# First layer of a four-layer kernel: products of tiles 0 and 1 interleaved over eight PSUM banks, with VectorE's order in tiles 1 and 2 and the place of the first down product changed

## Chip, cores and metric

The kernel runs on one core of a Trainium2 chip. The metric is the device time of one execution in microseconds (us). The kernel before takes 749.59 us, the median of 3 runs (749.37 to 749.69).

## What is computed

Four conditioned layers are applied in turn to x of 64 x 64 tokens of 256 features (4096 tokens), with one condition vector of 64 numbers per batch of 64 tokens. The change is in the first layer alone, a gated product with quantised activations and weights:

```
scale = cond @ norm_w.T + 1.0
ms = jnp.mean(x * x, axis=-1, keepdims=True)
h = x * (scale[:, None, :] * jax.lax.rsqrt(ms + EPS))
u = h @ up_w.T
val, gate = jnp.split(u, 2, axis=-1)
h = val * jax.nn.gelu(gate, approximate=False)
hq = h + jax.lax.stop_gradient(act_quant(h) - h)
wq = down_w + jax.lax.stop_gradient(weight_quant(down_w) - down_w)
y = hq @ wq.T
return y + x
```

The second layer is attention and a gated product, the third an adapter whose weights are made from the condition, the fourth a layer norm with a shift from the condition.

## The kernel before, in words

The program for each engine is written out by hand, with semaphores between engines. The first layer (`layer0`) works on 32 tiles (N) of 128 tokens. For each tile:

- GpSimd (POOL) scales the tile and splits it in a high and a low part (`split_tile`: xs L356, xs_hi L362, xs_lo L364, then semaphore xs_ready), and makes rstd0 from the tile's squares (`row_scale`, L371 and L373).
- TensorE (PE) multiplies by up_hi and up_lo (`up_chunk`, L435). A tile has four pieces of 512 columns in the order UP_ORDER: gate and value of the first half (j = 0), gate and value of the second (j = 1). Each piece takes three products, high by high, high by low and low by high, each of two matmuls, so 24 matmuls a tile. up_done counts halves.
- ScalarE (ACT) takes the gelu of the gate (`gate`, L552) and squares the tokens of a tile two ahead (`square_tokens`, L516), for which they must have been loaded.
- VectorE (DVE) multiplies gelu by the value into h (`gated`, L659, then h_done), finds the largest magnitude (`largest`, L667 to L671), rounds into q (`quantise`, L622 and L626, then q_done), and later adds the down product to the tokens as y (`add_tokens`, L614).
- SyncE (SP) issues the loads. From tile 4 on its order for tile s is: transpose of q of tile s - 3 (L272), w1_stage (L262), tokens of tile s (L259), tokens_again (L279). For tile 4 the first of these waits for q_done 2, which is q of tile 1.
- PE makes the down product of a tile (`down`, L452, 8 matmuls) two tiles later, and transposes y (`y_transposes`, L472) three tiles later.

Every engine runs its `body(s)` for s = 0, 1, 2, ... in `pipeline`; the first steps are unrolled, with special work in them. In step 0 and before it, the up weights arrive in four pieces: ACT rounds each to up_hi (L598) and DVE takes the rest as up_lo (L694). ACT sums the down weights' magnitudes (L575); in step 1 PE adds these over partitions (L488) and makes four condition vectors (L441), DVE derives the thresholds (`prepare_down`) and quantises the down weights in two steps, `below_minus_half` (L647) and `above_half` (L651). In step 2 PE makes three more condition vectors (L441), which ACT copies and turns into Tanh (L563, L589) behind its squares of the tokens of tile 4; before PE transposes the first y it waits for these (cond_done 4), because they share bank 7. y's product has bank 6.

The bank of a piece is 2j + part for every tile, so a tile can start on a half only when h of that half of the tile ahead has been made:

```
pe.wait_ge(Z["xs_ready"], t + 1)
wait(pe, Z["h_done"], 2 * s.at(1) + j + 1 if s.live(1) else 0)
```

Of the kernel before, what the change touches and what calls it, by code (L numbers as in the profile page):

```python
# [18 lines left out]
ACT = mybir.ActivationFunctionType  # L19
# [181 lines left out]
def layer0(nc, io, core, bank, sb, sem, early):  # L201
# [36 lines left out]
    stat_loaded, rstd_row = core["stat_loaded"], core["rstd_row"]  # L238
    norm_ps, down_ps, late_ps = bank[7][:, 0:DH * B], bank[7][:, 0:1], bank[7][:, DH * B:4 * DH * B]
    loaded_up, tokens_loaded, stage_loaded = ([sem(f"{n}{i}") for i in range(4)] for n in ("loaded_up", "tokens_loaded", "stage_loaded"))  # L240
# [7 lines left out]
    def sync_program(sp):  # L248
# [67 lines left out]
        load_up(3)  # L316
        load_tokens(first[1])
        sp.dma_start(down_f, io["down_t"]).then_inc(Z["loaded_down"], 16)
        sp.dma_start(core["ident"][:], io["ident"]).then_inc(Z["loaded_vecs"], 16)
        sp.dma_start(cond_w[:, (NORM + 1) * D:NV * D], io["cond_w"][:, (NORM + 1) * D:NV * D]).then_inc(Z["loaded_cond"], 16)  # L320
        sp.dma_start(vecs[:, 0:13], io["vecs"]).then_inc(Z["loaded_vecs"], 16)
        load_x(256, 512, "loaded_x1")
        for s in first:
# [75 lines left out]
    def gpsimd_program(pool):  # L399
        def body(s):  # L400
            if s.live(1):
                row_scale(pool, s, 1)
            split_tile(pool, s)
            if s.last(0):
                row_scale(pool, s, 0)
            w1_low(pool, s)
            if s.last(-1):
                attention_input(nc, pool, core, Step(0, 0, 1), 0)
                attention_input(nc, pool, core, Step(0, 0, 1), 1)
            if s.last(0):  # L410
                attention_input(nc, pool, core, Step(0, 0, 1), 2)
                attention_input(nc, pool, core, Step(1, 1, 1), 0)
                attention_input(nc, pool, core, Step(1, 1, 1), 1)
            row_scales(pool, s)
# [5 lines left out]


    def up_chunk(pe, s, j):

        t, k = s.at(0), s.slot(0, 2)
        if j == 0:
            pe.wait_ge(Z["xs_ready"], t + 1)
        wait(pe, Z["h_done"], 2 * s.at(1) + j + 1 if s.live(1) else 0)
        for part in (1, 0):
            at = part * FF + j * 512
            piece = UP_ORDER.index((j, part)) + 1  # L430
            for n, (a, b) in enumerate(((0, 0), (1, 0), (0, 1)) if s.first() else SPLITS):
                if s.first() and n != 1:
                    pe.wait_ge(Z["up_lo_done" if b else "up_hi_done"], piece)
                for d in range(DH):
                    last = nc.tensor.matmul(bank[2 * j + part][:, :], (xs_hi, xs_lo)[a][:, k, d, :], up[b][:, d, at:at + 512],  # L435
                                            start=n == d == 0, stop=n == 2 and d == DH - 1)
        last.then_inc(Z["up_done"], 1)
# [38 lines left out]
    def tensor_program(pe):  # L476
# [5 lines left out]
        def body(s):  # L482
            up_chunk(pe, s, 0)
            up_chunk(pe, s, 1)
            if s.first_tile(1):
                pe.wait_ge(Z["down_sum"], 1)
                pe.wait_ge(Z["norm_done"], 1)
                nc.tensor.matmul(down_ps, core["ones"][:], wscale[:, 0:1], start=True, stop=True).then_inc(Z["down_total"], 1)  # L488
                pe.wait_ge(Z["loaded_cond"], 16)
                for v in (GAMMA1, BETA1, ALPHA1, GAMMA2):  # L490
                    last = cond_vector(pe, v, bank[5][:, (v - GAMMA1) * DH * B:])
                last.then_inc(Z["cond_ready"], 1)
            y_transposes(pe, s)
            if s.first_tile(2):
# [3 lines left out]
                last.then_inc(Z["cond_ready"], 1)  # L498
            down(pe, s)

# [44 lines left out]
    def scalar_program(act):  # L545
        def gate(s, j):
            act.wait_ge(Z["up_done"], 2 * s.at(0) + j + 1)
            if j == 0:
                act.wait_ge(Z["rstd0_done"], s.at(0) + 1)
            wait(act, Z["h_done"], 2 * s.at(1) + j + 1 if s.live(1) else 0)  # L550
            hold(act, Z["passed"])
            nc.scalar.activation(gelu[:, j, :], bank[2 * j + 1][:, :], ACT.Gelu,  # L552
                                 scale=rstd0[:, bass.ds(s.at(0), 1)]).then_inc(Z["gelu_done"], 1)
# [12 lines left out]
        def body(s):  # L566
# [6 lines left out]
            if s.first():  # L573
                act.wait_ge(Z["loaded_down"], 16)
                nc.scalar.activation(stat[:, T // 2:T], down_f, ACT.Abs, accum_out=wscale[:, 0:1]).then_inc(Z["down_sum"], 1)  # L575
            if s.first_tile(1):
                w1_high(s, 1)
                square_tokens(act, s, -1)
            if not s.last(0) and not s.first():
                w1_high(s)  # L580
            if s.live(-2) and not s.first():
                square_tokens(act, s, -2)
            if s.first_tile(1):
                cond_vectors(GAMMA1, 4, bank[5], 1)
            if s.first_tile(2):
# [47 lines left out]
    def vector_program(ve):  # L633
# [20 lines left out]
        def gated(s, j):  # L654
            t, k = s.at(0), s.slot(0, 2)
            ve.wait_ge(Z["gelu_done"], 2 * t + j + 1)
            if j == 0:
                wait(ve, Z["q_done"], s.at(1))
            nc.vector.scalar_tensor_tensor(out=h[:, k, j * 512:(j + 1) * 512], in0=bank[2 * j][:, :], scalar=rstd0[:, bass.ds(t, 1)],  # L659
                                           in1=gelu[:, j, :], op0=ALU.mult, op1=ALU.mult).then_inc(Z["h_done"], 1)  # L660
# [12 lines left out]
        def body(s):  # L673
            add_tokens(ve, s)
            quantise(ve, s)
            gated(s, 0)
            if s.first_tile(1):
                prepare_down()
                below_minus_half()
            y_scale(ve, s)  # L680
            gated(s, 1)
            if s.first_tile(1):
                above_half()
            if s.last(0):
# [1372 lines left out]
```

## Time and profile before

| | us |
|---|---|
| Median of 3 runs | 749.59 |
| The profiled execution | 748.37 |
| Its span | 746.6 |
| PE busy | 730.2 (98%) |
| DVE busy | 518.1 (69%) |
| POOL busy | 419.5 (56%) |
| ACT busy | 363.4 (49%) |

The span is the time between the first and the last recorded event of the profiled execution. Busy counts leave out waiting and the issue of transfers. The granted clock of TensorE was 0.997 of full speed over the whole span. A matmul's recorded end is modelled, and matmuls overlap.

### The profile page before, as it was taken

The numbers are of one execution on the slowest core, as the hardware profiler recorded it, in microseconds if no ns is written. First come the engines' busy times: TensorE is split into PE (matmuls) and PEld (weight loads), VectorE is DVE, ScalarE is ACT, GpSimd is POOL, SyncE is SP. The second block draws the span as 40 slices with busy tenths as digits, with TensorE's granted clock in tenths as the row PEclk, the third lists the DMA queues.
The fourth block names the chain that finished last, engine by engine and source line by source line (L and its number), as shares of the span: only waits on it lengthen the run. The fifth ranks groups of instructions, "written<-read, shape, count | busy, mean of one in ns | idle before, by whom it ended". The sixth has DMA issues, their size and how long they took to land.

```text
span 746.6 us, 18077 instructions
## 1 busy us (share of the span) xinstructions
PE 730.2 (98%) x6406; PEld 597.5 (80%) x6406; DVE 518.1 (69%) x805; ACT 363.4 (49%) x719; POOL 419.5 (56%) x408
## 2 busy tenths in 40 slices
PE   8999999999999899999999999999999999999996
PEld 6888888888888799999988777677677767778884
DVE  3977778777789988888985464646655565553467
ACT  4444444444447687888875323333333332322585
POOL 4756646655678888999987533424242423320244
PEclk9999999999999999999999999999999999999998
DMA  8955344444433010000004355476757777759953
GB/s 244 296 108 107 86 118 106 106 120 117 99 81 74 12 36 3 2 1 0 2 4 127 76 185 178 153 243 204 203 181 246 215 223 222 243 161 389 387 179 129
DMA packets 80810, 105.69 MB, mean 142 GB/s; under 512 B 39760, under 2 KB 53168, under 8 KB 80624
## 3 DMA queue, kind: packets, MB, share of 16 engines
q1 hardware_dynamic: 79600, 103.32, 46.9%
q10 hardware_dynamic: 1152, 1.59, 1.0%
q8 instruction: 38, 0.62, 0.3%
q14 instruction: 20, 0.16, 0.1%
HBM read 75.23 MB, written 21.26 MB: 129 GB/s over the span
## 4 chain that ended last, share of the span: by engine, by line
PE 90%; DVE 3%; POOL 3%; issue 2%; DMA 1%; ACT 1%; SPq 0%; DVEq 0%; POOLq 0%; ACTq 0%
PE banks L435 23%; PE banks L1202 22%; PE banks L1232 12%; PE banks L1048 5%; PE banks L1254 4%; PE banks L1125 4%; PE banks L452 4%; PE banks L1083 3%; PE banks L1166 3%; PE banks L1141 2%; PE banks L1863 2%; PE banks L1107 2%; PE banks L1833 2%; DMA early<-in_up_t 1%; PE banks L1855 1%
## 5 line engine op out<-in xcount | busy, mean ns | idle before, releaser
L1584 DVE TENSOR_TENSOR g<-banks,silu 128x512 f32<-128x512 f32 x64 | 44.1, 689 | 79.3 <-PE banks L1202 52.0
L1424 ACT ACTIVATE g_hi<-g 128x512 fp32r<-128x512 f32 x64 | 40.4, 631 | 97.8 <-DVE g L1584 96.7
L1588 DVE TENSOR_TENSOR g_lo<-g,g_hi 128x512 fp32r<-128x512 f32 x64 | 55.0, 859 | 47.5 <-ACT g_hi L1424 47.5
L1418 ACT ACTIVATE silu<-banks 128x512 f32<-128x512 f32 x64 | 38.2, 597 | 97.9 <-PE banks L1202 97.9
L435 PE MATMUL banks<-up_hi,xs_hi 128*128 128x512 f32 x256 | 81.9, 401 | 1.3 <-POOL xs_lo L364 0.8
L435 PE MATMUL banks<-up_lo,xs_hi 128*128 128x512 f32 x256 | 79.5, 391 | 0.5 <-DVE up_lo L694 0.5
L435 PE MATMUL banks<-up_hi,xs_lo 128*128 128x512 f32 x256 | 79.2, 391 | 0.0
L1202 PE MATMUL banks<-mlp_in_hi,w_hi 128*128 128x512 f32 x252 | 78.8, 394 | 0.0
L1202 PE MATMUL banks<-mlp_in_lo,w_hi 128*128 128x512 f32 x252 | 78.0, 391 | 0.0
L1202 PE MATMUL banks<-mlp_in_hi,w_lo 128*128 128x512 f32 x252 | 77.8, 390 | 0.0
L659 DVE SCALAR_TENSOR_TENSOR h<-banks,rstd,gelu 128x512 f32<-128x512 f32 x64 | 47.9, 748 | 35.4 <-ACT gelu L552 35.2
L552 ACT ACTIVATE gelu<-banks,rstd 128x512 f32<-128x512 f32 x64 | 43.9, 686 | 43.7 <-PE banks L435 36.0
L940 POOL TENSOR_TENSOR p_sb<-p_sb,rec 128x1024 f32<-128x1024 f32 x32 | 60.7, 1905 | 7.7 <-DVE rec L1543 7.7
L724 POOL TENSOR_TENSOR mlp_in_lo<-mlp_in,mlp_in_hi 128x1024 fp32r<-128x1024 f32 x8 | 19.9, 2490 | 77.2 <-ACT mlp_in_hi L731 77.2
L435 PEld LDWEIGHTS banks<-up_lo,xs_hi 128*128 128x128 f32 x256 | 47.8, 188 | 11.7 <-DVE up_lo L694 1.7
L435 PEld LDWEIGHTS banks<-up_hi,xs_lo 128*128 128x128 f32 x256 | 48.1, 188 | 10.4
L1202 PEld LDWEIGHTS banks<-mlp_in_lo,w_hi 128*128 128x128 f32 x252 | 47.3, 188 | 10.7
L1202 PEld LDWEIGHTS banks<-mlp_in_hi,w_hi 128*128 128x128 f32 x252 | 47.2, 188 | 10.8
L1202 PEld LDWEIGHTS banks<-mlp_in_hi,w_lo 128*128 128x128 f32 x252 | 47.3, 188 | 10.3
L1232 PE MATMUL banks<-g_hi,w_hi 128*128 128x512 f32 x128 | 52.7, 412 | 2.3 <-DVE y_alpha L1597 1.7
L714 POOL TENSOR_TENSOR mlp_in<-x_sb,stat 128x1024 f32<-128x1024 f32 (+1 forms) x8 | 19.6, 2445 | 61.0 <-DMA stat<-rstd_row 43.1
L435 PEld LDWEIGHTS banks<-up_hi,xs_hi 128*128 128x128 f32 x256 | 45.6, 188 | 10.2 <-POOL xs_lo L364 0.9
(224 smaller groups left out, 1806.3 us busy)
## 6 DMA issues: line engine op xcount, KB each, us to landing
gen_hyper<-in_gen_t SPq DMA_DIRECT2D x32, 512.0 KB, 4.5
gen_made<-base_w SPq DMA_DIRECT2D x64, 256.0 KB, 4.4
adapter_w<-gen_made SPq DMA_DIRECT2D x64, 256.0 KB, 4.4
tokens<-in_x_tok SPq DMA_DIRECT2D x32, 128.0 KB, 2.4
w_stage<-in_w_t SPq DMA_DIRECT2D x32, 128.0 KB, 2.4
tokens_again<-in_x_tok SPq DMA_DIRECT2D x32, 128.0 KB, 2.3
weight_slot<-adapter_w SPq DMA_DIRECT2D x4, 1024.0 KB, 8.9
x_sb<-in_x_t SPq DMA_DIRECT2D x7, 512.0 KB, 7.1
```

The lines of the kernel that those rows point to most:

```text
L435: last = nc.tensor.matmul(bank[2 * j + part][:, :], (xs_hi, xs_lo)[a][:, k, d, :], up[b][:, d, at:at + 512], start=n == d == 0, stop=n == ...
L452: last = nc.tensor.matmul(y_ps, qt[:, s.slot(2, 2), f, :], downq[:, f, :], start=f == 0, stop=f == FC - 1)
L552: nc.scalar.activation(gelu[:, j, :], bank[2 * j + 1][:, :], ACT.Gelu, scale=rstd0[:, bass.ds(s.at(0), 1)]).then_inc(Z["gelu_done"], 1)
L659: nc.vector.scalar_tensor_tensor(out=h[:, k, j * 512:(j + 1) * 512], in0=bank[2 * j][:, :], scalar=rstd0[:, bass.ds(t, 1)], in1=gelu[:, j, ...
L940: nc.gpsimd.tensor_tensor(pu, pu, rec[:, two, :].unsqueeze(2).to_broadcast([P, 16, L]), ALU.mult).then_inc(A["norm_done"], 1)
L1048: last = nc.tensor.matmul(ps[:, m * GTA:(m + 1) * GTA], w1[a][:, w + d * D + m * P:w + d * D + (m + 1) * P], ha[b][k][:, d, :], start=n == ...
L1202: last = nc.tensor.matmul(chunk_bank(s, f, i)[:, :], w1[a][:, at:at + P], hs[b][k][:, d, :], start=n == d == 0, stop=n == 2 and d == DH - 1)
L1232: last = nc.tensor.matmul(bank[5 + m][:, :], w1[a][:, at:at + P], gs[b][:, f % 2, :], start=f == n == 0, stop=f == FC - 1 and n == 2)
L1418: nc.scalar.activation(silu[:, f % 2, :], chunk_bank(s, f, 0)[:, :], ACT.Silu).then_inc(S["silu_done"], 1)
L1424: nc.scalar.activation(gs[0][:, f % 2, :], g[:, f % 2, :], ACT.Copy).then_inc(S["g_hi_done"], 1)
L1584: nc.vector.tensor_tensor(g[:, f % 2, :], chunk_bank(s, f, 1)[:, :], silu[:, f % 2, :], ALU.mult).then_inc(S["g_done"], 1)
L1588: nc.vector.tensor_tensor(gs[1][:, f % 2, :], g[:, f % 2, :], gs[0][:, f % 2, :].bitcast(FP32), ALU.subtract).then_inc(S["g_ready"], 1)
```

## The change

In step 0 PE runs the 48 matmuls of tiles 0 and 1 in a hand-written order (`first_two_tiles`). Tile 1 has banks 4 to 7 of its own and no wait for h; its first two products stand between the high and the low products of tile 0's second piece. To feed it, POOL splits tile 1 directly after tile 0, ahead of the rstd of tile 0. The total and the first four condition vectors get other banks (3 and 2), and wait for h_done 2. Tile 2 is back in banks 0 to 3, and its second half waits for the copy of the condition vectors, which ACT makes earlier in step 1. The down product of tile 0 moves from the end of step 2 to between the two halves of tile 3. On DVE `below_minus_half` goes behind the second h of tile 1, `above_half` goes from step 1 into step 2 between the two h of tile 2, and quantising tile 1 goes behind them. On SP the load of x for tiles 2 and 3 goes ahead of the down weights.

```diff
--- before.py
+++ after.py
@@ -236,7 +236,7 @@
     lines_ps, last_lines_ps = bank[7][0:4, DH * P:DH * P + P], bank[3][0:4, 0:P]
     row_squares, row_rstd = core["rows"]
     stat_loaded, rstd_row = core["stat_loaded"], core["rstd_row"]
-    norm_ps, down_ps, late_ps = bank[7][:, 0:DH * B], bank[7][:, 0:1], bank[7][:, DH * B:4 * DH * B]
+    norm_ps, down_ps, norm_four_ps, late_ps = bank[7][:, 0:DH * B], bank[3][:, 0:1], bank[2], bank[7][:, DH * B:4 * DH * B]
     loaded_up, tokens_loaded, stage_loaded = ([sem(f"{n}{i}") for i in range(4)] for n in ("loaded_up", "tokens_loaded", "stage_loaded"))
     qt_loaded, again_loaded = ([sem(f"{n}{i}") for i in range(2)] for n in ("qt_loaded", "again_loaded"))
     names = ("loaded_norm loaded_cond loaded_vecs loaded_down loaded_x0 loaded_x1 loaded_x norm_ready norm_done cond_ready cond_done "
@@ -315,11 +315,11 @@
         load_up(2)
         load_up(3)
         load_tokens(first[1])
+        load_x(256, 512, "loaded_x1")
         sp.dma_start(down_f, io["down_t"]).then_inc(Z["loaded_down"], 16)
         sp.dma_start(core["ident"][:], io["ident"]).then_inc(Z["loaded_vecs"], 16)
         sp.dma_start(cond_w[:, (NORM + 1) * D:NV * D], io["cond_w"][:, (NORM + 1) * D:NV * D]).then_inc(Z["loaded_cond"], 16)
         sp.dma_start(vecs[:, 0:13], io["vecs"]).then_inc(Z["loaded_vecs"], 16)
-        load_x(256, 512, "loaded_x1")
         for s in first:
             load_stage(s)
         for s in first[2:4]:
@@ -400,7 +400,10 @@
         def body(s):
             if s.live(1):
                 row_scale(pool, s, 1)
-            split_tile(pool, s)
+            if not s.first_tile(1):
+                split_tile(pool, s)
+            if s.first():
+                split_tile(pool, Step(1, 1, N))
             if s.last(0):
                 row_scale(pool, s, 0)
             w1_low(pool, s)
@@ -419,21 +422,68 @@
+    def up_bank(s, j, part):
+
+        return bank[2 * j + part + (4 if s.first_tile(1) else 0)]
+
+    def up_product(s, piece, a, b, start, stop):
+
+        (j, part), k = UP_ORDER[piece], s.slot(0, 2)
+        at = part * FF + j * 512
+        for d in range(DH):
+            last = nc.tensor.matmul(up_bank(s, j, part)[:, :], (xs_hi, xs_lo)[a][:, k, d, :], up[b][:, d, at:at + 512],
+                                    start=start and d == 0, stop=stop and d == DH - 1)
+        return last
+
+    def first_two_tiles(pe):
+
+        first, second = Step(0, 0, N), Step(1, 1, N)
+
+        def with_high(s, piece):
+            up_product(s, piece, 0, 0, True, False)
+            up_product(s, piece, 1, 0, False, False)
+
+        def with_low(s, piece):
+            return up_product(s, piece, 0, 1, False, True)
+
+        pe.wait_ge(Z["xs_ready"], 1)
+        pe.wait_ge(Z["up_hi_done"], 1)
+        with_high(first, 0)
+        pe.wait_ge(Z["up_lo_done"], 1)
+        with_low(first, 0)
+        pe.wait_ge(Z["up_hi_done"], 2)
+        with_high(first, 1)
+        pe.wait_ge(Z["xs_ready"], 2)
+        with_high(second, 0)
+        pe.wait_ge(Z["up_lo_done"], 2)
+        with_low(first, 1).then_inc(Z["up_done"], 1)
+        with_low(second, 0)
+        pe.wait_ge(Z["up_hi_done"], 3)
+        with_high(first, 2)
+        pe.wait_ge(Z["up_hi_done"], 4)
+        with_high(first, 3)
+        pe.wait_ge(Z["up_lo_done"], 3)
+        with_low(first, 2)
+        pe.wait_ge(Z["up_lo_done"], 4)
+        with_low(first, 3).then_inc(Z["up_done"], 1)
+        with_high(second, 1)
+        with_low(second, 1).then_inc(Z["up_done"], 1)
+        with_high(second, 2)
+        with_low(second, 2)
+        with_high(second, 3)
+        with_low(second, 3).then_inc(Z["up_done"], 1)
+
     def up_chunk(pe, s, j):
 
-        t, k = s.at(0), s.slot(0, 2)
+        t = s.at(0)
         if j == 0:
             pe.wait_ge(Z["xs_ready"], t + 1)
-        wait(pe, Z["h_done"], 2 * s.at(1) + j + 1 if s.live(1) else 0)
+        pe.wait_ge(Z["h_done"], 2 * s.at(1) + j + 1)
+        if s.first_tile(2) and j == 1:
+            pe.wait_ge(Z["cond_done"], 1)
         for part in (1, 0):
-            at = part * FF + j * 512
-            piece = UP_ORDER.index((j, part)) + 1
-            for n, (a, b) in enumerate(((0, 0), (1, 0), (0, 1)) if s.first() else SPLITS):
-                if s.first() and n != 1:
-                    pe.wait_ge(Z["up_lo_done" if b else "up_hi_done"], piece)
-                for d in range(DH):
-                    last = nc.tensor.matmul(bank[2 * j + part][:, :], (xs_hi, xs_lo)[a][:, k, d, :], up[b][:, d, at:at + 512],
-                                            start=n == d == 0, stop=n == 2 and d == DH - 1)
+            for n, (a, b) in enumerate(SPLITS):
+                last = up_product(s, UP_ORDER.index((j, part)), a, b, n == 0, n == 2)
         last.then_inc(Z["up_done"], 1)
 
     def cond_vector(pe, v, ps):
@@ -480,15 +530,20 @@
                 nc.tensor.matmul(bank[5][:, 0:P], core["ones"][:], core["ones"][:], start=True, stop=True)
 
         def body(s):
-            up_chunk(pe, s, 0)
-            up_chunk(pe, s, 1)
+            if s.first():
+                first_two_tiles(pe)
+            elif not s.first_tile(1):
+                up_chunk(pe, s, 0)
+                if s.first_tile(3):
+                    down(pe, Step(2, 2, N))
+                up_chunk(pe, s, 1)
             if s.first_tile(1):
+                pe.wait_ge(Z["h_done"], 2)
                 pe.wait_ge(Z["down_sum"], 1)
-                pe.wait_ge(Z["norm_done"], 1)
                 nc.tensor.matmul(down_ps, core["ones"][:], wscale[:, 0:1], start=True, stop=True).then_inc(Z["down_total"], 1)
                 pe.wait_ge(Z["loaded_cond"], 16)
                 for v in (GAMMA1, BETA1, ALPHA1, GAMMA2):
-                    last = cond_vector(pe, v, bank[5][:, (v - GAMMA1) * DH * B:])
+                    last = cond_vector(pe, v, norm_four_ps[:, (v - GAMMA1) * DH * B:])
                 last.then_inc(Z["cond_ready"], 1)
             y_transposes(pe, s)
             if s.first_tile(2):
@@ -496,7 +551,8 @@
                 for v in (BETA2, ALPHA2, TAR):
                     last = cond_vector(pe, v, late_ps[:, (v - BETA2) * DH * B:])
                 last.then_inc(Z["cond_ready"], 1)
-            down(pe, s)
+            if not s.first_tile(2):
+                down(pe, s)
 
         pe.wait_ge(Z["ones_done"], 1)
         warm(WARM)
@@ -549,7 +605,7 @@
                 act.wait_ge(Z["rstd0_done"], s.at(0) + 1)
             wait(act, Z["h_done"], 2 * s.at(1) + j + 1 if s.live(1) else 0)
             hold(act, Z["passed"])
-            nc.scalar.activation(gelu[:, j, :], bank[2 * j + 1][:, :], ACT.Gelu,
+            nc.scalar.activation(gelu[:, j, :], up_bank(s, j, 1)[:, :], ACT.Gelu,
                                  scale=rstd0[:, bass.ds(s.at(0), 1)]).then_inc(Z["gelu_done"], 1)
 
         def w1_high(s, lag=0):
@@ -574,14 +630,13 @@
                 act.wait_ge(Z["loaded_down"], 16)
                 nc.scalar.activation(stat[:, T // 2:T], down_f, ACT.Abs, accum_out=wscale[:, 0:1]).then_inc(Z["down_sum"], 1)
             if s.first_tile(1):
+                cond_vectors(GAMMA1, 4, norm_four_ps, 1)
                 w1_high(s, 1)
                 square_tokens(act, s, -1)
             if not s.last(0) and not s.first():
                 w1_high(s)
             if s.live(-2) and not s.first():
                 square_tokens(act, s, -2)
-            if s.first_tile(1):
-                cond_vectors(GAMMA1, 4, bank[5], 1)
             if s.first_tile(2):
                 cond_vectors(BETA2, 2, late_ps, 2)
                 act.wait_ge(Z["loaded_vecs"], 32)
@@ -656,7 +711,7 @@
             ve.wait_ge(Z["gelu_done"], 2 * t + j + 1)
             if j == 0:
                 wait(ve, Z["q_done"], s.at(1))
-            nc.vector.scalar_tensor_tensor(out=h[:, k, j * 512:(j + 1) * 512], in0=bank[2 * j][:, :], scalar=rstd0[:, bass.ds(t, 1)],
+            nc.vector.scalar_tensor_tensor(out=h[:, k, j * 512:(j + 1) * 512], in0=up_bank(s, j, 0)[:, :], scalar=rstd0[:, bass.ds(t, 1)],
                                            in1=gelu[:, j, :], op0=ALU.mult, op1=ALU.mult).then_inc(Z["h_done"], 1)
 
         def largest(s):
@@ -672,15 +727,21 @@
 
         def body(s):
             add_tokens(ve, s)
-            quantise(ve, s)
+            if not s.first_tile(2):
+                quantise(ve, s)
             gated(s, 0)
             if s.first_tile(1):
                 prepare_down()
-                below_minus_half()
-            y_scale(ve, s)
+            if s.first_tile(2):
+                above_half()
+            else:
+                y_scale(ve, s)
             gated(s, 1)
             if s.first_tile(1):
-                above_half()
+                below_minus_half()
+            if s.first_tile(2):
+                quantise(ve, s)
+                y_scale(ve, s)
             if s.last(0):
                 add_tokens(ve, Step(N, 0, N))
             largest(s)
```

On DVE, the place around the end of step 1 and step 2 (h is the product of gelu and value, small the scale of a row, downq the quantised down weights), from the second h of tile 1 to the reduction of tile 2. Before:

```order
L659 SCALAR_TENSOR_TENSOR h<-banks,rstd,gelu 128x512
L651 SCALAR_TENSOR_TENSOR downq<-early,wscale,downq 128x2048
L667 TENSOR_REDUCE small<-h 128x1
L669 TENSOR_SCALAR small<-small 128x1
L671 RECIPROCAL small<-small 128x1
L622 TENSOR_SCALAR h<-h,small 128x1024
L626 TENSOR_SCALAR q<-h 128x1024
L659 SCALAR_TENSOR_TENSOR h<-banks,rstd,gelu 128x512
L631 TENSOR_SCALAR small<-small,wscale 128x1
L659 SCALAR_TENSOR_TENSOR h<-banks,rstd,gelu 128x512
L667 TENSOR_REDUCE small<-h 128x1
```

Now:

```order
L714 SCALAR_TENSOR_TENSOR h<-banks,rstd,gelu 128x512
L702 TENSOR_SCALAR downq<-early,wscale 128x2048
L722 TENSOR_REDUCE small<-h 128x1
L724 TENSOR_SCALAR small<-small 128x1
L726 RECIPROCAL small<-small 128x1
L714 SCALAR_TENSOR_TENSOR h<-banks,rstd,gelu 128x512
L706 SCALAR_TENSOR_TENSOR downq<-early,wscale,downq 128x2048
L714 SCALAR_TENSOR_TENSOR h<-banks,rstd,gelu 128x512
L677 TENSOR_SCALAR h<-h,small 128x1024
L681 TENSOR_SCALAR q<-h 128x1024
L686 TENSOR_SCALAR small<-small,wscale 128x1
L722 TENSOR_REDUCE small<-h 128x1
```

The first row of each piece is h of the second half of tile 1. The comparison of two inputs (L651, now L706) has moved from before the reduction of tile 1 to between the two h of tile 2, and the rounding of tile 1 (h by small, then q) from before both h of tile 2 to behind them.

On POOL, the first two tiles' splits. Before:

```order
L356 TENSOR_TENSOR xs<-x_sb,cond_vectors 128x256
L362 CAST xs_hi<-xs 128x256
L364 TENSOR_TENSOR xs_lo<-xs,xs_hi 128x256
L371 TENSOR_TENSOR ss<-ss,wscale 128x1
L373 TENSOR_TENSOR rstd<-ss,wscale 128x1
L356 TENSOR_TENSOR xs<-x_sb,cond_vectors 128x256
L362 CAST xs_hi<-xs 128x256
L364 TENSOR_TENSOR xs_lo<-xs,xs_hi 128x256
```

Now:

```order
L356 TENSOR_TENSOR xs<-x_sb,cond_vectors 128x256
L362 CAST xs_hi<-xs 128x256
L364 TENSOR_TENSOR xs_lo<-xs,xs_hi 128x256
L356 TENSOR_TENSOR xs<-x_sb,cond_vectors 128x256
L362 CAST xs_hi<-xs 128x256
L364 TENSOR_TENSOR xs_lo<-xs,xs_hi 128x256
L371 TENSOR_TENSOR ss<-ss,wscale 128x1
L373 TENSOR_TENSOR rstd<-ss,wscale 128x1
```

The split of tile 1 stands directly behind that of tile 0, and rstd of tile 0 behind both.

On SP, from the first transpose (q of tile 0) to the tokens of tile 4; the order of these rows is the same in both programs, and the semaphore that a row waits for stands in brackets:

```order
L272 DMA_TRANSPOSE qt<-q 128x8x128 [waits z_q_done]
L279 DMA tokens_again<-in_x_tok 128x256
L250 DMA x_sb<-in_x_t 128x2x512 [waits z_up_done]
L250 DMA x_sb<-in_x_t 128x2x512 x2
L272 DMA_TRANSPOSE qt<-q 128x8x128 [waits z_q_done]
L262 DMA w_stage<-in_w_t 128x256 [waits z_w1_lo_done]
L259 DMA tokens<-in_x_tok 128x256 [waits z_squared_done]
```

Nothing has moved here: the second transpose (q of tile 1) still stands ahead of the weights and the tokens of tile 4, which are the last two rows.

## Rows read from the trace of the kernel before

**Rows 1.** Windows view: busy us (x instructions) per engine, PEclk, DMA share, GB/s

```profile
0.00:20.00 20.00, 17.25 (x83) 13.97 (x84) 8.17 (x9) 9.44 (x13) 7.69 (x16) 1.00 0.85 246
...
20.00:40.00 20.00, 20.00 (x112) 16.83 (x111) 17.26 (x32) 8.20 (x24) 15.21 (x21) 1.00 0.98 283
```

**Rows 2.** Chain that ended last, first 45 us: start us, us, what

```profile
13.38 1.67 DVE up_lo L694
...
15.09 7.58 PE banks L435 x32
...
24.70 5.69 PE banks L435 x24
...
39.42 5.48 PE banks L435 x24
```

**Rows 3.** Timeline, PE, tiles 0 and 1: start us, us, engine line op, [idle before]

```profile
11.56 0.62 PE L435 MATMUL banks<-up_hi,xs_lo 128*128 128x512 f32 x2
...
13.40 0.73 PE L435 MATMUL banks<-up_hi,xs_hi 128*128 128x512 f32 x2 [0.51 <-ACT up_hi L598]
...
16.58 0.61 PE L435 MATMUL banks<-up_lo,xs_hi 128*128 128x512 f32 x2
```

**Rows 4.** Timeline, POOL and DVE, 8 to 14 us

```profile
7.38 0.62 POOL L356 TENSOR_TENSOR xs<-x_sb,cond_vectors 128x256 f32<-128x256 f32 x1 [6.42 <-DVE cond_vectors L690]
...
8.65 0.72 POOL L364 TENSOR_TENSOR xs_lo<-xs,xs_hi 128x256 fp32r<-128x256 f32 x1
...
9.24 1.23 DVE L694 TENSOR_TENSOR up_lo<-early,up_hi 128x1024 fp32r<-128x1024 f32 x1 [2.01 <-ACT up_hi L598]
...
9.69 0.83 POOL L371 TENSOR_TENSOR ss<-ss,wscale 128x1 f32<-128x1 f32 x1 [0.32 <-ACT squared L516]
...
10.87 1.23 DVE L694 TENSOR_TENSOR up_lo<-early,up_hi 128x1024 fp32r<-128x1024 f32 x1 [0.41 <-ACT up_hi L598]
...
11.14 1.43 POOL L356 TENSOR_TENSOR xs<-x_sb,cond_vectors 128x256 f32<-128x256 f32 x1
...
12.74 0.40 POOL L362 CAST xs_hi<-xs 128x256 fp32r<-128x256 f32 x1 [0.17 <-POOL xs L356]
...
13.22 0.73 POOL L364 TENSOR_TENSOR xs_lo<-xs,xs_hi 128x256 fp32r<-128x256 f32 x1
```

**Rows 5.** Timeline, DVE and ACT around tiles 0 to 3

```profile
18.05 0.75 DVE L659 SCALAR_TENSOR_TENSOR h<-banks,rstd,gelu 128x512 f32<-128x512 f32 x1 [1.23 <-ACT gelu L552]
...
25.34 2.34 DVE L651 SCALAR_TENSOR_TENSOR downq<-early,wscale,downq 128x2048 bf16<-128x2048 f32 x1
...
28.20 0.69 ACT L552 ACTIVATE gelu<-banks,rstd 128x512 f32<-128x512 f32 x1 [2.81 <-POOL rstd L373]
...
29.23 0.75 DVE L622 TENSOR_SCALAR h<-h,small 128x1024 f32<-128x1024 f32 x1
...
30.02 1.11 DVE L626 TENSOR_SCALAR q<-h 128x1024 bf16<-128x1024 f32 x1
...
31.05 0.74 DVE L659 SCALAR_TENSOR_TENSOR h<-banks,rstd,gelu 128x512 f32<-128x512 f32 x1
...
42.80 0.69 DVE L626 TENSOR_SCALAR q<-h 128x1024 bf16<-128x1024 f32 x1
```

**Rows 6.** Timeline, SP, ACT, DVE and PE, 31 to 39 us

```profile
33.22 0.43 SPq L259 DMA_DIRECT2D tokens<-in_x_tok  x1
...
36.15 0.42 ACT L516 ACTIVATE squared<-tokens 128x256 f32<-128x256 f32 x1 [4.62 <-DMA tokens<-in_x_tok]
...
36.83 0.51 ACT L589 ACTIVATE cond_vectors<-banks,vecs 128x64 f32<-128x64 f32 x2
...
37.95 0.75 DVE L659 SCALAR_TENSOR_TENSOR h<-banks,rstd,gelu 128x512 f32<-128x512 f32 x1 [1.85 <-ACT gelu L552]
...
38.17 0.38 PE L472 MATMUL banks<-ident,y 128*128 128x128 f32 x2
```

**Rows 7.** DMA issues, 0 to 40 us: KB each, median us to landing

```profile
early<-in_down_t SPq DMA_DIRECT2D x1, 1024.0 KB, 11.0
```

## Prediction

> **What bounds the kernel now.** I read the windows first. TensorE (PE) is busy 17.25 us of the first 20 and all of the next 20, at a granted clock of 1.00 [rows 1], so there is nothing to win but the gaps of the first 20 us. The chain that ended last says the same in order of time: up to 15.04 us it runs through a load, ACT's rounding and DVE's up_lo; from 15.09 it is PE alone, 32 products in 7.58 us, that is 0.237 us each with the drain, to 22.67 [rows 2]. Tile 2 follows at 24.70, after the total and 16 small products of the condition vectors, and tile 4 at 39.42; one tile of 24 products takes 5.48 us, 0.228 each [rows 2]. I use the start of tile 4 as the clock of the whole change: behind it the two programs are alike, PE repeats tiles without gaps, and a microsecond at 39.42 is a microsecond at the end.
>
> Then the gaps themselves. Two products of the second piece start at 11.56; the products of piece 3 wait for ACT until 13.40, 0.51 us of it shown as idle. Tile 0 is finished at 16.58 + 0.61 = 17.19 [rows 3]. Work of tile 1 could lie in these gaps; that is what the new PE order offers.
>
> **Step 1: when can tile 1 begin?** Its first products stand ahead of the low product of piece 2 now, so PE comes to them after 10 products: 11.56 + 2 x 0.228 = 12.02. They wait for xs_lo of tile 1 on POOL. xs_lo of tile 0 ends at 8.65 + 0.72 = 9.37, so the moved xs can be issued at about 9.5. It doesn't run there. Beside DVE's up_lo (9.24 to 10.47) a one-column POOL sum took 0.83 us and ended at 10.52; beside the next up_lo (10.87 to 12.10) xs took 1.43 us where it takes 0.62 alone, and ended 0.47 after DVE [rows 4]. By these rows: xs ends at 10.47 + 0.47 = 10.94; xs_hi (0.40) is issued 0.17 later, at 11.11, inside the second up_lo, which has slipped by some 0.07 to 12.17, and ends about 12.5; xs_lo, 0.08 later, takes 0.73 and ends at 13.33 [rows 4]. Between bounds of 12.02 (no delay; PE isn't there earlier) and 13.6 (xs misses the gap between the two up_lo) I take 13.35. So PE stands idle from 12.02 to 13.35, with the low product of piece 2 ready behind the wait.
>
> The Trainium skill (SBUF — State Buffer, section on the two separate sides) says that VectorE and GpSimd share a port pair as an exclusive lock, which the one that starts first holds for the whole instruction. The rows above agree as to POOL. By the rule to the letter xs would end at 11.09 and xs_lo at about 13.5, 0.15 later than my sum.
>
> **Step 2: PE.** From 13.35 all inputs of tile 0 come in time (up_hi of piece 3 was ready at 13.38, where DVE began on it [rows 2]). 20 products finish tile 0: 13.35 + 0.1 for the restart (0.73 against 0.62 for a pair [rows 3]) + 20 x 0.237 = 18.2, which is 1.0 later than 17.19. 38 products finish both tiles: 13.45 + 9.0 = 22.45, 0.2 to 0.3 earlier than 22.67. Had xs_lo been ready at 12.02, these would be 16.85 (0.35 earlier) and 21.1 (1.5 earlier). Tile 2 starts 2.03 later as before, at 24.4. The total and the condition products go to free banks; their two new waits (h_done 2, DVE at about 19.8, and cond_done 1 before the second half of tile 2) end before PE comes.
>
> **Step 3: VectorE.** h of tile 0, second half, starts at 18.05 [rows 5] and moves with the end of tile 0 to 19.05. From there DVE works through. Before, quantising tile 1 starts at 29.23, ends at 30.02 + 1.11 = 31.13, and the first half of tile 2's h starts at 31.05 [rows 5]. Now the order is h(2,0), the 2.34 us comparison above_half, h(2,1), and only then the two quantising steps. Taking above_half (2.34) and quantising (1.9) out from ahead of 31.05 and adding the 1.0, DVE is free for h(2,0) at about 27.8. But its gelu needs tile 2's first 12 products: in the order of before gelu(2,0) began at 28.20, held by POOL's rstd [rows 5]; now the products end at 24.4 + 12 x 0.237 + 0.1 = 27.35, gelu takes 0.69, so h(2,0) starts at 28.2. Then 0.74 + 2.34 + 0.74 + 0.75 + 0.69 (q beside an idle POOL; 1.11 beside a busy one [rows 5]), less some 0.07 of overlap at each, gives 33.3 for the end of q of tile 1. That is 2.2 us later than 31.13.
>
> **Step 4: what hangs on q of tile 1.** This is the step that decides. SP issues in order: the transpose of q(1) waits for q_done 2, and behind it stand a weight load and the tokens of tile 4, issued at 33.22. ACT waited 4.62 us for these tokens, squared them at 36.15, and only behind that come the last condition vectors (second Tanh ends about 37.34) and gelu(3,0). h(3,0) starts at 37.95 and ends at 38.70; the transposes of y(0), which need those vectors, run at 38.17 [rows 6]; tile 4's first product needs h(3,0) and starts at 39.42 [rows 2]. So the slack was 0.8 us for the vectors and 0.7 us for h(3,0). The distance from the end of q(1) to the end of h(3,0) is 38.70 - 31.13 = 7.57 us of issue, transfer, ACT and DVE, none of it PE's.
>
> Shifted by 2.2 the vectors are ready at 39.5 and h(3,0) at 40.9. PE, without waiting, would be through tile 3 and its first down product (now placed between the halves of tile 3) near 38.3, so it idles about 1.2 us before the transposes of y(0), and tile 4 starts at about 41.0: 1.5 to 1.6 later than 39.42. The 0.2 to 0.3 us gained in step 2 is inside this number, not beside it. Behind it h, q and the transfers of tiles 4 and 5 have over 2 us of room, so it is paid once.
>
> Bounds. Below: tile 1 ready at 12.02 makes DVE start 1.35 earlier, and the transfer, issued 33.22 with a landing of 2.9 us behind a queue that will have emptied, may be 0.2 to 0.4 quicker; the sum falls to about zero. Above: the rstd of tile 2, which waits on POOL behind the comparison and its own tokens, could hold gelu(2,0) 0.3 longer, q may take 1.11 instead of 0.69, and a slower transfer adds some 0.5: plus 2.6.
>
> The down-product's move by itself costs nothing: the same 8 products, with qt of tile 0 long landed. The second x load (0.26 MB) goes ahead of down_t: at 246 GB/s [rows 1] that is 1.1 us, so down_t lands at 19.2 instead of 7.15 + 11.0 [rows 7], about where ACT comes to it (gelu(0,1) ends near 19.05); its sum is done by 21.2, and PE asks for it at 22.4. The hold on rstd of tile 0 behind the moved split delays gelu(0,0) to about 16.4, before gelu(0,1) needs ACT.
>
> **The rivals.**
> (a) Faster: PE's gaps are filled and q(1) stays off the path. It decides if q of tile 1 ends before about 31.8 (31.13 plus the slack of 0.7). That needs POOL's split to run beside up_lo unhindered and DVE to lose nothing to the new order. The gap saved is then up to 1.5 us, 747.9 to 748.1. Against it: two extra halves of h (1.5 us) stand ahead of q(1) whatever PE does, and rows 4 show POOL held. Chance 0.09.
> (b) No difference that can be told: POOL is held less than I think, or DVE and the tokens gain from fewer collisions, and q(1) with what follows is 0.7 to 2.1 late, so that tile 4 starts up to 1.4 after 39.42: 749.6 to 751.0. Chance 0.3.
> (c) The interleave does not interleave, since POOL delivers tile 1 after piece 3 is there anyway. This is nearly my forecast for step 1; alone, with the chain of step 4 hidden by some cover that I don't see, it would give 749.3. Chance 0.07.
> (d) Slower by more: the upper bounds of step 4 together, 2.6 us, 752.2. Chance 0.1.
>
> **How the numbers follow.** The profiled execution took 748.37 us around a span of 746.6; the median of the runs is 749.59. I add 1.6 to both: 749.97 against the profile's own, and 751.2 as the forecast, with a chance of 0.44 for tile 4 starting 1.5 to 2.2 late. A measurement here can tell about 0.2%, 1.5 us, from no change, so slower means above 751.09; the forecast lies just beyond that, which is why (b) keeps so much. Slower 0.54 (the forecast and (d)), same 0.37 ((b) and (c)), faster 0.09 ((a)). The range goes from 748.9, which leaves most of (a) out, to 752.3, the upper bound of step 4.
>
> **What the changed profile would show.** Right, if POOL's xs_lo of tile 1 ends near 13.3 and PE is idle about a microsecond before it; if tile 0 ends near 18.2; if q of tile 1 ends near 33.3, ACT squares the tokens of tile 4 near 38.3, and PE stands before the transposes of y(0) near 38 to 39.5. Wrong, if tile 4 starts before 39.4, or if the tokens of tile 4 land before 37. A stall at the first products of tile 2 or at the down product would show a wait that I have put at nothing.

## The result and the profile after

The changed kernel takes 751.35 us, the median of 15 runs (749.55 to 752.34), beside 749.49 of the kernel before, again 15 runs. The ratio is 1.0022 with a 95% interval of 1.0015 to 1.0029: slower by 1.1 to 2.2 us, 1.6 by the ratio, 1.9 by the medians. The profiled execution took 751.8 us, its span is 750.0 (746.6 before).

The early timeline of the changed kernel, PE, POOL and DVE, answers to [rows 3, 4] (start us, us, what, in brackets the idle time before and who ended it):

```profile
9.20 1.60 POOL L356 TENSOR_TENSOR xs<-x_sb,cond_vectors 128x256 f32<-128x256 f32 x1
...
10.97 0.40 POOL L362 CAST xs_hi<-xs 128x256 fp32r<-128x256 f32 x1 [0.17 <-POOL xs L356]
...
11.45 1.66 POOL L364 TENSOR_TENSOR xs_lo<-xs,xs_hi 128x256 fp32r<-128x256 f32 x1
...
11.89 0.62 PE L434 MATMUL banks<-up_hi,xs_lo 128*128 128x512 f32 x2
...
13.15 0.73 PE L434 MATMUL banks<-up_hi,xs_hi 128*128 128x512 f32 x2 [0.64 <-POOL xs_lo L364]
...
16.91 1.07 PE L434 MATMUL banks<-up_lo,xs_hi 128*128 128x512 f32 x4
...
21.45 0.61 PE L434 MATMUL banks<-up_lo,xs_hi 128*128 128x512 f32 x2
...
22.53 1.66 PE L491 MATMUL banks<-cond_t,early 64*128 64x64 f32 x13 [0.35 <-DMA early<-in_cond_w]
```

POOL is held in xs (1.60 us) as forecast, and in xs_lo (1.66) where the forecast had it held in xs_hi; xs_lo of tile 1 ends at 13.11, and PE stood idle 0.64 us before it. Tile 0 ends at 17.98 (17.19 before), both tiles at 22.06 (22.67). A wait of 0.35 us for the condition weights is new.

The timeline from tile 2 to tile 4, which answers to [rows 5, 6]:

```profile
25.63 1.06 PE L434 MATMUL banks<-up_hi,xs_lo 128*128 128x512 f32 x2
...
29.20 0.69 ACT L608 ACTIVATE gelu<-banks,rstd 128x512 f32<-128x512 f32 x1 [2.63 <-PE banks L434]
...
29.92 0.75 DVE L714 SCALAR_TENSOR_TENSOR h<-banks,rstd,gelu 128x512 f32<-128x512 f32 x1 [2.53 <-ACT gelu L608]
...
30.59 2.34 DVE L706 SCALAR_TENSOR_TENSOR downq<-early,wscale,downq 128x2048 bf16<-128x2048 f32 x1
...
32.85 0.74 DVE L714 SCALAR_TENSOR_TENSOR h<-banks,rstd,gelu 128x512 f32<-128x512 f32 x1
...
34.28 0.69 DVE L681 TENSOR_SCALAR q<-h 128x1024 bf16<-128x1024 f32 x1
```

```profile
37.05 0.43 SPq L259 DMA_DIRECT2D tokens<-in_x_tok  x1
...
39.26 0.61 PE L434 MATMUL banks<-up_hi,xs_lo 128*128 128x512 f32 x2
39.41 0.42 ACT L572 ACTIVATE squared<-tokens 128x256 f32<-128x256 f32 x1 [6.47 <-DMA tokens<-in_x_tok]
...
40.09 0.51 ACT L644 ACTIVATE cond_vectors<-banks,vecs 128x64 f32<-128x64 f32 x2
...
40.74 0.41 PE L522 MATMUL banks<-ident,y 128*128 128x128 f32 x2 [0.87 <-ACT cond_vectors L644]
...
41.21 0.75 DVE L714 SCALAR_TENSOR_TENSOR h<-banks,rstd,gelu 128x512 f32<-128x512 f32 x1 [1.96 <-ACT gelu L608]
...
42.11 0.70 PE L434 MATMUL banks<-up_hi,xs_hi 128*128 128x512 f32 x2
```

q of tile 1 ends at 34.28 + 0.69 = 34.97. SP issues tile 4's tokens at 37.05, ACT squares them at 39.41 after 6.47 us of waiting, and PE, through tile 3 at 39.87, stands until the condition vectors are there at 40.6. Tile 4 starts at 42.11, 2.69 later than at 39.42 [rows 2], and ends at 47.82 against 44.90, 2.9 later, since PE has to start anew behind its wait.

One thing in it was not forecast. A pair of products takes 1.06 us at 25.63 instead of 0.62. The windows view of the changed kernel gives the granted clock (third number from the end):

```profile
24.00:26.00 2.00, 2.00 (x10) 1.68 (x10) 2.00 (x4) 1.44 (x5) 0.39 (x1) 0.82 1.06 387
26.00:28.00 2.00, 2.00 (x6) 1.57 (x5) 1.32 (x3) 0.56 (x3) 1.76 (x5) 0.50 1.84 241
28.00:30.00 2.00, 2.00 (x8) 1.60 (x8) 0.08 (x1) 0.69 (x1) 1.92 (x4) 0.82 0.53 91
30.00:32.00 2.00, 2.00 (x11) 1.40 (x10) 2.00 (x2) 0.06 (x1) 0.61 (x2) 1.00 1.10 370
```

From some point after 25 to some point before 29 us the clock was at 0.50, the lower of its two levels (1.2 of 2.4 GHz). The first 12 products of tile 2 take 4.54 us there, as the chain of waits has it (line below), where a restarted half tile at full clock takes about 3.0. So by this estimate 1.5 of the 2.9 us are the clock's in this execution, and 1.4 the chain's.

```profile
24.52 4.54 PE banks L434 x12
...
30.67 2.26 DVE downq L706
...
37.05 2.23 DMA tokens<-in_x_tok
...
42.11 5.71 PE banks L434 x24
```

### The profile page after: what moved, and what is told of

It is laid out like the page before. It is cut to its first block, busy times and chain, and to the rows that moved or that the text cites. A ratio compares the mean times of both kernels' runs of the same rounds, so it can differ in the third digit from the quotient of the medians.

```text
span 750.0 us, 18077 instructions
## 1 busy us (share of the span) xinstructions
PE 732.5 (98%) x6406; PEld 598.6 (80%) x6406; DVE 518.4 (69%) x805; ACT 363.6 (48%) x719; POOL 415.1 (55%) x408
## 4 chain that ended last, share of the span: by engine, by line
PE 87%; DVE 4%; POOL 3%; DMA 2%; issue 2%; SPq 1%; ACT 1%; DVEq 0%; ACTq 0%; POOLq 0%
PE banks L1263 22%; PE banks L434 21%; PE banks L1293 12%; PE banks L1109 5%; PE banks L1315 4%; PE banks L1186 4%; PE banks L502 3%; PE banks L1144 3%; PE banks L1227 3%; PE banks L1202 2%; PE banks L1924 2%; PE banks L1168 2%; PE banks L1894 2%; DMA early<-in_cond_w 2%; PE banks L1916 1%
## 5 line engine op out<-in xcount | busy, mean ns | idle before, releaser
L1649 DVE TENSOR_TENSOR g_lo<-g,g_hi 128x512 fp32r<-128x512 f32 x64 | 56.5, 883 | 47.5 <-ACT g_hi L1485 47.5
```

The costliest lines, as they stand in the source:

```text
L1649: nc.vector.tensor_tensor(gs[1][:, f % 2, :], g[:, f % 2, :], gs[0][:, f % 2, :].bitcast(FP32), ALU.subtract).then_inc(S["g_ready"], 1)
```

## The experiments

Theory 1 is that of the prediction: the loss comes through q of tile 1, SP's queue, the tokens of tile 4 and ACT. Theory 2: the fall of the clock costs the time and the chain rides along. All ratios are to the kernel before, timed on the same chip in the same rounds.

**Undoing the chain.** On SP, tile 4's tokens are issued ahead of the last x loads (and left out in step 4, a second edit that the diff doesn't show):

```diff
                 load_again(Step(3, 3, N))
+                sp.wait_ge(Z["squared_done"], 1)
+                load_tokens(Step(4, 0, N))
         pipeline(sp, N, 14, 4, body, start=4, stop=N)
```

> The changed kernel, with the load of tile 4's tokens issued right behind the first transpose on SP, no longer behind the transpose of tile 1's q. Theory 1 (the chain q(1), SP, tokens, ACT's condition vectors and gelu(3,0) sets the start of tile 4): ACT squares these tokens before 34 us, the idle 0.87 us ahead of the transposes of y(0) is gone, tile 4 starts about 1.1 us earlier than 42.11 in a profile with the same clock, and the median falls from 751.35 to about 750.2. Theory 2 (the granted clock, at half from about 25.3 to 28.6 us, costs PE 1.5 us by itself and the chain is a passenger): the median stays within 0.4 us of 751.3, since tile 4 can't start before PE is through tile 3.

Measured: 749.23 us, ratio 1.0002 (0.9993 to 1.0011), 1.0 us less than the 750.2 expected. All of the loss goes with one transfer. Its profile happened to have a fall of the clock at the same place and as long (25.0 to 28.2 us, 25.2 to 28.8 above), which makes it a clean pair with the one above:

```profile
32.79 0.40 ACT L575 ACTIVATE squared<-tokens 128x256 f32<-128x256 f32 x1
...
34.23 0.69 DVE L684 TENSOR_SCALAR q<-h 128x1024 bf16<-128x1024 f32 x1
...
39.22 0.62 PE L437 MATMUL banks<-up_hi,xs_lo 128*128 128x512 f32 x2
...
39.68 0.38 PE L525 MATMUL banks<-ident,y 128*128 128x128 f32 x2
...
40.69 0.71 PE L437 MATMUL banks<-up_hi,xs_hi 128*128 128x512 f32 x2
```

The tokens are squared at 32.79, q of tile 1 ends at 34.92, as late as before, and PE passes the transposes at 39.68 without a wait. Tile 4 starts at 40.69 and ends at 46.40 in its chain, 1.42 earlier than 47.82 at the same clock. Theory 1 holds, and theory 2 as the only cause falls.

**One part of the change alone.** VectorE's new order in the kernel before:

```diff
-            quantise(ve, s)
+            if not s.first_tile(2):
+                quantise(ve, s)
             gated(s, 0)
...
             gated(s, 1)
+            if s.first_tile(1):
+                below_minus_half()
+            if s.first_tile(2):
+                quantise(ve, s)
+                y_scale(ve, s)
```

> The kernel before with VectorE's new order alone; PE, POOL, ACT and SP as before. Theory 1: h(2,0) waits for gelu(2,0) at 28.9, the comparison, h(2,1) and quantising follow, q of tile 1 ends near 34.0 (31.13 before), h(3,0) near 41.5, and tile 4 starts about 2.1 us later than 39.42: 751.6. Theory 2: no half clock near 26 us without PE's new order, so 749.5.

Measured: 751.12 us (5 runs), ratio 1.0033 (1.0020 to 1.0047), with the clock at 1.00 through the first 60 us of the profile. The order alone does it, by the same wait:

```profile
33.61 0.69 DVE L626 TENSOR_SCALAR q<-h 128x1024 bf16<-128x1024 f32 x1
...
38.77 0.42 ACT L516 ACTIVATE squared<-tokens 128x256 f32<-128x256 f32 x1 [6.53 <-DMA tokens<-in_x_tok]
...
40.10 0.41 PE L472 MATMUL banks<-ident,y 128*128 128x128 f32 x2 [1.07 <-ACT cond_vectors L589]
...
40.57 0.75 DVE L659 SCALAR_TENSOR_TENSOR h<-banks,rstd,gelu 128x512 f32<-128x512 f32 x1 [2.30 <-ACT gelu L552]
```

q of tile 1 ends at 34.30 (34.0 expected), h(3,0) at 41.32 (41.5), and tile 4 starts at 41.46, 2.04 later than 39.42 (2.1 expected).

> The kernel before with tile 4's tokens issued early on SP, a control. Theory 1: the chain ended 0.7 us before PE needed it, so tile 4 starts at 39.4 still and the time is that of before within 0.3 us (749.2 to 749.8), though ACT's 4.62 us wait for the tokens goes. Theory 2 says the same. A gain of more would show a second place where these tokens count.

The control: the same SP edit in the kernel before gives 749.27 us, ratio 1.0005 (0.9995 to 1.0015); one of its 12 runs took 1459.53 us, which the median leaves aside. With the old order the transfer is hidden.

**The old order in the new kernel.** VectorE's body as before, all else as changed:

> The changed kernel with VectorE's old order in tiles 1 and 2 (both comparisons in step 1, quantising tile 1 ahead of tile 2's h). Theory 1: q of tile 1 ends near 32 instead of 34.97, tokens of tile 4 are squared near 37, h(3,0) is there before 40, and the median is 749.7 to 750.3. Theory 2: no gain from the order of VectorE, 751.0 to 751.5, with the clock at half near 26 us as before.

Measured: 751.23 us, ratio 1.0030 (1.0021 to 1.0040). That is not what theory 1 said (749.7 to 750.3). Its profiled execution was the quickest of ten (748.82), with the clock at 1.00 through the first 60 us. It had q of tile 1 at 31.4 and tile 4 at 39.95, as expected, but also a new wait of PE, 1.19 us for h(2,0) ahead of tile 3. The chain of waits has tile 3's first half behind it:

```profile
32.22 2.98 PE banks L434 x12
```

Of the other nine only one has a mean clock over 0.996, and it took 749.79 us; the eight at or below average 751.5. The same kernel with the early tokens:

> The changed kernel with VectorE's old order and tile 4's tokens early. With the old order alone the profile showed PE waiting 1.2 us for h(2,0) ahead of tile 3, since quantising tile 1 stands before it on DVE, and the chain through q(1) had room. So by theory 1 the tokens' early load brings little here: ratio to before within 0.05% of the old order's 1.0030, or down to 1.0015 if the executions in the middle were set by a late q(1). If it falls to 1.0000 or less, the wait for h(2,0) costs nothing and theory 1 has to explain the old order's 751.2 as the same chain.

Measured: 751.43 us, ratio 1.0016 (1.0002 to 1.0030), at the lower end of what was expected. PE's timeline and the windows of that kernel:

```profile
32.73 0.98 PE L437 MATMUL banks<-up_hi,xs_hi 128*128 128x512 f32 x2 [1.18 <-DVE h L717]
33.51 1.05 PE L437 MATMUL banks<-up_lo,xs_hi 128*128 128x512 f32 x2
...
36.68 0.63 PE L437 MATMUL banks<-up_hi,xs_lo 128*128 128x512 f32 x2
```

```profile
32.00:34.00 2.00, 1.27 (x4) 1.01 (x5) 1.97 (x4) 0.38 (x2) 1.21 (x3) 0.74 1.04 383
34.00:36.00 2.00, 2.00 (x6) 1.58 (x5) 0.94 (x3) 0.00 (x0) 0.71 (x2) 0.50 1.16 335
```

Here quantising tile 1 and both comparisons stand ahead of h(2,0), and PE, which no longer has a down product before tile 3, waits 1.18 us for it. Right behind that wait the clock falls to 0.50, and half a tile takes 4.58 us in the chain of waits instead of 2.98 in the execution without a fall. All 12 executions have a mean granted clock of 0.996 or less, against 8 of 15 of the changed kernel and 12 of 29 of the kernel before in the same rounds. So VectorE's new order is not idle: it spares this wait, and paid with a later q. That the wait brings the fall is not shown: the profile of the old order alone has the same wait and no fall, and took less time than any of the other nine.

**The clock and the gaps.** Three edits to the changed kernel: the second x load back behind vecs on SP; with the early tokens too; and the low product of tile 0's second piece ahead of tile 1's high ones:

```diff
-        pe.wait_ge(Z["xs_ready"], 2)
-        with_high(second, 0)
         pe.wait_ge(Z["up_lo_done"], 2)
         with_low(first, 1).then_inc(Z["up_done"], 1)
+        pe.wait_ge(Z["xs_ready"], 2)
+        with_high(second, 0)
```

> The changed kernel with SP's second load of x back behind the condition weights and vecs. In the profile of the change PE waited 0.35 us for the condition weights ahead of the 16 small products, ACT 0.59 us for the down weights, and the granted clock was at half from 25.3 to 28.6 us. Theory 2a (the late condition weights thin out PE's work before the fall and so bring it): no wait, clock 1.00 throughout, gelu(2,0) 1.5 us earlier, and the median falls by 0.6 to 1.3 us against the change (about 750.0). Theory 2b (the fall has nothing to do with that wait): median within 0.4 us of the change's 751.0 to 751.4, clock still at half in the profile.

Measured: 751.76 us, ratio 1.0023 (1.0012 to 1.0034). PE's wait for the condition weights came all the same (0.24 us), so the place of the x load isn't its cause. The clock fell, for the longer stretch from 24.5 to 31.3 us, in a profile that is the slowest of its 13 executions (755.16). But the edit brought a wait of its own: x of tile 2 landed at 22.8, and PE stood idle for 1.74 us, from 24.3 to 26.0, for tile 2's xs_lo on POOL. The chain of waits:

```profile
24.12 1.84 POOL xs_lo L364
...
26.01 8.22 PE banks L434 x24
```

The clock fell inside that wait, so the run can't tell whether the place of the load has to do with the fall in the changed kernel.

> The changed kernel with both: tile 4's tokens early on SP and the second load of x back. Theory 1 with 2a: PE has no idle stretch between tile 2 and tile 5 and no clock fall: 748.0 to 748.4, about 1 us below the kernel before. Theory 1 with 2b: like the tokens alone, equal to before within 0.4 us (749.0 to 749.5).

Measured: 749.32 us, ratio 0.9991 (0.9980 to 1.0003), as expected without a gain from the place of the x load.

> The changed kernel with that low product moved alone. Theory 1: the two tiles end 0.4 us earlier and tile 0's h, hence q of tile 1 and the start of tile 4, at most 0.4 us earlier: 750.6 to 751.2. If the order of these products also sets whether the clock falls (theory 2), the clock stays at 1.00 near 26 us and the median is nearer 750.0.

Measured: 750.62 us, ratio 1.0010 (0.9998 to 1.0021), at the lower end of what was expected; the interval doesn't tell a gain of 0.4 us from none. Its profile (749.17 us) has no fall in the first 60 us, and PE still waits 1.26 us before the transposes: the chain without the clock.

> The changed kernel with three products of ones by ones (0.19 us each in the profile, as in the warm-up) behind the total, where PE waits for the condition weights before the 16 small products; they add nothing to the result. The granted clock fell to half near 25 us in three profiles so far (the change, its version with early tokens, its version with x back), and in each PE had a gap ahead of those small products; it did not in seven profiles without the gap. Theory 2a (the gap ahead of the small products brings the fall): clock 1.00 near 26 us in the profile, no execution with a mean clock of 0.995 or less, and the median 0.3 to 0.8 us below the change's (ratio to before 1.0012 to 1.0018), since the added 0.4 us of PE hides in its idle stretch before the transposes of y(0). Theory 2b (the fall comes from elsewhere): falls in a third of the executions as in the change, ratio 1.0020 to 1.0030.

```diff
+                for _ in range(3):
+                    nc.tensor.matmul(bank[0][:, 0:P], core["ones"][:], core["ones"][:], start=True, stop=True)
                 pe.wait_ge(Z["loaded_cond"], 16)
```

Measured: 751.37 us, ratio 1.0023 (1.0008 to 1.0039), and 4 of 12 executions at a mean clock of 0.996 or less. Theory 2a falls in this form: with no gap ahead of the small products low mean clocks remain, and the profile has a fall at another place. In this profile PE had waited 1.81 us for its first product, and the clock was at 0.50 from 12 to 15 us:

```profile
12.00:14.00 2.00, 2.00 (x6) 1.51 (x6) 1.38 (x1) 0.92 (x2) 1.92 (x3) 0.50 1.09 417
```

Nothing sets the falls seen in five profiles apart. PE was idle for 1.81 us ending 1.5 us ahead of one, for 1.18 us right ahead of another and for 0.35 us some 2.7 us ahead of that of the changed kernel; one began inside an idle stretch of 1.74 us; ahead of that with the early tokens no idle time of 0.2 us or more stands between 12.93 and the fall at 25.0. And profiles without a fall have gaps as long: 1.81 us before the first product in the first run of the last version below, 1.19 us in the old order's. What brings a fall stays open.

**Towards a version that beats both.**

> As the last, and the low product of tile 0's second piece moved ahead of the high products of tile 1, into the stretch in which PE waits for POOL's xs_lo (0.64 us idle in the change's profile, 12.5 to 13.15 us). Expected: tile 0 and tile 1 end 0.4 to 0.5 us earlier, 0.3 to 0.5 us below the last kernel: 747.6 to 748.0. If POOL's xs_lo comes before DVE's second up_lo ends, no gain.

Measured: 749.12 us, ratio 0.9990 (0.9978 to 1.0002). The 0.3 to 0.5 us expected below the last kernel (747.6 to 748.0) did not come: the ratio is that without the moved product, 0.9991.

> The changed kernel with tile 4's tokens early and the low product of tile 0's second piece in the gap, x left where the change put it. Theory 1: tokens alone gave 1.0002 and the low product takes 0.4 us more away: ratio 0.9990 to 0.9998. With x early, tile 2's split has more room than in the version that moved it back (0.9990), so not slower than that by more than 0.05%.

Measured: 748.74 us, ratio 0.9989 (0.9976 to 1.0002), about as expected. The chain of waits shows what the interleave was worth with q of tile 1 off the path:

```profile
10.96 11.26 PE banks L437 x48
...
22.34 1.99 PE banks L494 x16
...
39.17 5.47 PE banks L437 x24
```

48 products run in 11.26 us without a gap. But the first product comes at 10.96 here, since POOL's xs_hi of tile 0 took 1.44 us beside up_lo (0.40 alone), and in the next run of the same kernel at 9.27, with 1.0 us of waits for the up weights behind it. Tile 4 ends at 44.64 and at 44.58, 0.3 earlier than 44.90. That is within what two profiles differ by: in the two versions with x back it ends at 44.13 and 44.89, behind first products at 8.94 and 10.91. The start of the first product decides as much as the filled gaps.

> The same kernel as n_tok_low, timed again, since its interval (0.9976 to 1.0002) still held no change. By theory 1 the gaps of the first 22 us are worth about 0.7 us once q of tile 1 is off the path: ratio 0.9985 to 0.9995. If it comes out at 1.0000 or above, the interleave is worth nothing even without the chain.

Measured: 748.70 us, ratio 0.9994 (0.9985 to 1.0003). Two timings at 0.9989 and 0.9994, and neither interval excludes no change: the best version is level with the kernel before, or up to 0.2% faster. That the interleave is worth anything is not shown by them.

## Why the prediction was right

**Step 1** gave the time, in part by luck: 13.11 for the end of xs_lo where 13.33 stood. PE's gap was 0.64 us and not 1.3, since PE came to it at 12.5 and not at 12.02. Loads landed at other times than before, so up_lo 2 began at 11.30 and POOL was held in xs_lo rather than in xs_hi. The sum came out close by another collision of the same kind: xs_lo, issued at 11.45 beside an up_lo that ran from 11.30 to 12.52, ended 0.59 after it. The Trainium skill (SBUF — State Buffer, section on the two separate sides) says that the one of VectorE and GpSimd that starts first holds the shared port pair for the whole instruction, and the other blocks. The trace agrees to within 0.14 us: alone xs_lo takes 0.73. In the ten other profiles with this order on POOL, xs_lo of tile 1 ends anywhere from 11.57 to 13.87.

**Step 2** held: tile 0 ends at 17.98 (18.2 forecast), both tiles at 22.06 (22.45).

**Step 3** was right in its mechanism and off in one term. h(2,0) was to start at 28.2 and started at 29.92. The sum took 12 products at 0.237 us; in this execution most of them ran at half clock, some 1.5 us longer. From there its durations hold: 34.97 - 29.92 = 5.05 us, 5.1 forecast. Without the fall q of tile 1 would by estimate end near 33.4, the forecast being 33.3.

**Step 4** held in its mechanism, with a smaller distance: from the end of q(1) to the end of h(3,0) it is 41.96 - 34.97 = 6.99 us and not 7.57, because the tokens took 2.36 us from issue to use (2.93 before), 0.57 quicker where the lower bound allowed 0.2 to 0.4. It is no accident of this profile: the four others in which PE waits before the transposes have 6.94 to 7.33. This term was 0.2 to 0.6 too large. PE's wait before the transposes was 0.87 us for a forecast of 1.2. Tile 4 started at 42.11 and not at 41.0: 1.7 for the late h(2,0), less 0.6 for the quicker chain. PE's wait of 0.35 us for the condition weights was put at nothing, and is inside the first of these. Without a fall, and with the low product moved, tile 4 starts at 40.03 and ends at 45.74, 0.8 later than 44.90. Behind the end of tile 4 the span runs 702.2 us, 701.7 before; over the twelve other profiles this rest lies between 701.6 and 702.8, so it is scatter between executions and not the change.

The executions point the same way. The 7 of the changed kernel with a mean clock over 0.996 average 750.7 us, 1.2 above the kernel before; the 8 at or below average 751.6. The mark is a rough one: the mean takes in the end of the span too, where PE is idle and the clock low, and the changed kernel with early tokens and x back has 0.996 without a fall before that. The kernel before is not free of low clocks either: in the rounds of the experiments 26 of its 106 executions stand at or below 0.996, 12 of them at 750.9 to 753.7 us. So the measured 1.6 to 1.9 is put together, as far as is known, of 1.2 to 1.4 from the chain and a part from falls of the clock, of which it is not shown how much the change adds. Only the first was in the forecast of 1.6, with a distance that was too large. That the number lay so close is in part luck.

"The down product's move costs nothing" held for the product. But it took cover away from tile 3's first wait, for h(2,0), which the old VectorE order then shows. This is read from the place of the wait: no run puts the down product back.

## What to carry to other kernels

Follow a delayed result through the queues that are issued in order, not only to its direct reader: here, in the kernel before, the down product that reads q of tile 1 comes 7.4 us behind it (31.13, 38.55), but a transfer waited behind its transpose, and ScalarE's and TensorE's next work behind that transfer. A reordering that fills gaps on the bounding engine should be tried together with the move of such a load ahead of the wait. Here that took the loss away (1.0022 to 1.0002) but gave no gain that can be told: the best version was timed at 0.9989 and 0.9994, with no change inside both intervals.

## What was not expected of the hardware

The granted clock of TensorE fell from 1.00 to 0.50 for 3 to 7 us in five of fourteen profiles, in the first 37 us each time, with half a tile of products costing 1.5 to 1.6 us more (4.54 and 4.58 for about 3.0). A kernel with a wait of 1.18 us ahead of tile 3 had a mean clock of 0.996 or less in 12 of 12 executions, but the kernel before had it in 12 of 29 in the same rounds, and a profile with a wait of 1.19 us at the same place had no fall. A comparison of two kernels by a us or so should therefore be made between executions of like clock, as the pair of profiles above.
